# Attention: key rows loaded through GpSimd's queue, and a three-level split without GpSimd

## The reference, cut to what matters

```
# layer 0, 16 heads of 16, causal, S = 2048, batch 2
q, k, v = x @ Wq.T + bq, x @ Wk.T + bk, x @ Wv.T + bv
w = softmax(q k^T / sqrt(16) + alibi, causal);  y = w v;  x += y @ Wo.T + bo
# layer 1: two score maps per head
y = (softmax(q1 k1^T) - lam * softmax(q2 k2^T)) v;  y = layernorm per head;  x += y @ Wc
```

## Time and profile before

| | us |
|---|---|
| Time, median of 3 runs (lowest, highest) | 6747.85 (6737.48, 6751.71) |
| The profiled execution, its own time | 6750.49 |
| Its span in the trace | 6748.4 |
| PE, DVE, ACT, POOL busy | 5221.8, 3307.6, 2556.6, 1576.2 |

### The profile page before, as it was taken

The page is one execution under the profiler, slowest core; times in us unless marked ns, Lnnn a source line. Parts: engine busy times, 40 slices in busy tenths (PEclk is TensorE's granted clock), DMA queues, the critical chain, the costliest instruction groups (busy, mean ns, idle before and its releaser), DMA issues. The chain is left out here.

```text
span 6748.4 us, 94042 instructions
## 1 busy us (share of the span) xinstructions
PE 5221.8 (77%) x30108; PEld 2792.5 (41%) x30112; DVE 3307.6 (49%) x4783; ACT 2556.6 (38%) x5006; POOL 1576.2 (23%) x1276
## 2 busy tenths in 40 slices
PE   6566558888787566489968688888888888977997
PEld 3454223333225355248943233333323333344686
DVE  7411646666545621311157566666666666543011
ACT  2311116655561311122221265556555665612221
POOL 2488200000001288333323000000000001002332
PEclk9678769999898687789989699999999999988998
DMA  2476431112103277408945111111111111011498
GB/s 93 114 149 131 144 95 42 42 48 62 56 27 111 74 153 148 115 0 295 315 162 161 47 34 45 52 38 34 46 51 37 34 47 50 16 62 35 160 314 274
DMA packets 454295, 660.14 MB, mean 98 GB/s; under 512 B 97984, under 2 KB 308992, under 8 KB 448672
## 3 DMA queue, kind: packets, MB, share of 16 engines
q1 hardware_dynamic: 383232, 544.50, 25.8%
q0 software_dynamic: 70656, 110.44, 8.1%
HBM read 489.33 MB, written 164.20 MB: 97 GB/s over the span
## 5 line engine op out<-in xcount | busy, mean ns | idle before, releaser
L1670 DVE TENSOR_REDUCE ea_mx<-ea_psA 128x1 f32<-128x1024 f32 (+7 forms) x1280 | 1317.0, 1061 | 691.8 <-PE ea_psA L1535 484.4
L1652 ACT ACTIVATE ea_pr<-ea_psB 128x512 f32<-128x512 f32 (+3 forms) x2560 | 1229.5, 535 | 928.6 <-PE ea_psB L1557 508.1
L1532 PE MATMUL ea_psA<-ea_kx,ea_qx 99*128 99x512 bf16 (+3 forms) x2560 | 728.5, 362 | 284.3 <-DMA ea_kx<-in_c_k 255.0
L1670 DVE TENSOR_REDUCE ba_mx<-ba_psA 128x1 f32<-128x1024 f32 (+7 forms) x640 | 657.2, 1061 | 379.3 <-PE ba_psA L1535 279.9
L1557 PE MATMUL ea_psB<-ea_qx,ea_kx 99*128 99x512 bf16 (+3 forms) x2560 | 782.2, 354 | 29.1 <-issue 21.1
L1652 ACT ACTIVATE ba_pr<-ba_psB 128x512 f32<-128x512 f32 (+3 forms) x1280 | 610.7, 535 | 493.3 <-PE ba_psB L1557 259.4
L1572 PE MATMUL ea_psO<-ea_pr,ea_vx 128*32 128x512 f32 (+3 forms) x5120 | 610.5, 549 | 1.9 <-ACT ea_pr L1652 0.4
L1532 PE MATMUL ba_psA<-ba_kx,ba_qx 108*128 108x512 bf16 (+3 forms) x1280 | 370.5, 368 | 197.9 <-DMA ba_kx<-in_c_k 180.1
L1532 PEld LDWEIGHTS ea_psA<-ea_kx,ea_qx 99*128 99x128 bf16 x2560 | 217.5, 100 | 691.9 <-issue 378.5
L1504 POOL DMA_DIRECT2D ea_qx<-ea_mT x192 | 105.6, 557 | 1540.0 <-DVE ea_mT L1692 1515.8
L1557 PEld LDWEIGHTS ea_psB<-ea_qx,ea_kx 99*128 99x128 bf16 x2560 | 242.3, 99 | 500.9 <-ACT ea_pr L1652 315.0
(11 more groups left out here) (524 smaller groups left out, 8248.3 us busy)
## 6 DMA issues: line engine op xcount, KB each, us to landing
de_wg<-in_L_rg SPq DMA_DIRECT2D x64, 512.0 KB, 4.6
de_wu<-in_L_ru SPq DMA_DIRECT2D x64, 512.0 KB, 5.7
de_wd<-in_L_rd SPq DMA_DIRECT2D x64, 512.0 KB, 7.2
fe_wg<-in_L_rg SPq DMA_DIRECT2D x64, 512.0 KB, 4.6
fe_wu<-in_L_ru SPq DMA_DIRECT2D x64, 512.0 KB, 5.6
fe_wd<-in_L_rd SPq DMA_DIRECT2D x64, 512.0 KB, 7.0
ae_w<-in_L_w SPq DMA_DIRECT2D x64, 384.0 KB, 3.8
ce_w<-in_L_w SPq DMA_DIRECT2D x64, 384.0 KB, 3.5
```

The source lines that it names most:

```text
L1532: last = nc.tensor.matmul(psA[:, slot, at:at + n], qx[0:KB, s, hh, t * P:(t + 1) * P], kx[0:KB, s, hh, k:k + n], start=True, stop=not diag)
L1652: nc.scalar.activation(pr[:, j % 2, hh, off:BLK], psB[:, exp_slot(n, s), off:BLK], ACT.Exp).then_inc(s_exp, 1)
L1670: v.tensor_reduce(out, src, AX.X, ALU.max).then_inc(s_ar, 1)
```

## The change

Three edits.

1. The 14 key loads of a step (12 of levels, 2 of constants) leave SP and are issued by POOL, in the order 32, 16, 48 rows in each group. POOL issues them ahead of portion 1 of the step's maxima, behind the same wait for PE. SP issues all 14 query loads in one piece, then `vx`, then the inverses.
2. PE's one wait for both groups becomes one for the queries and one for the keys. The keys' semaphores now last over both attentions.
3. In the projections ACT reads `ps` twice, into `t32` and into the first level; DVE makes the remainder, the second level and the third. POOL does nothing there. ACT waits for the third level of two units earlier, where it waited for the second.

```
 # project_phase, ACT
-                    nc.scalar.activation(t32[:, k % 2, :], ps[:, k % 2, :], f, scale=mats[m][2],
+                    nc.scalar.activation(t32[:, k % 2, :], ps[:, k % 2, :], f, scale=mats[m][2], **a)
+
+                    act.wait_ge(s_out[k % NL], ((b * QB + i) * (nu // NL) + k // NL) * 16)
+                    nc.scalar.activation(lev[:, k % NL, 0], ps[:, k % 2, :], f, scale=mats[m][2],
 # project_phase, DVE
-                    nc.vector.tensor_copy(lev[:, v, 0], t32[:, u, :]).then_inc(s_c, 1)
+                    nc.vector.tensor_tensor(res[:, u, :], t32[:, u, :], lev[:, v, 0], ALU.subtract).then_inc(s_c, 1)
                     dve.wait_ge(s_c, base + n * 2 + 1)
-                    after(dve, s_lo, n, 2, first)
-                    nc.vector.tensor_tensor(res[:, u, :], t32[:, u, :], lev[:, v, 0], ALU.subtract).then_inc(s_c, 1)
+                    nc.vector.tensor_copy(lev[:, v, 1], res[:, u, :]).then_inc(s_c, 1)
                     dve.wait_ge(s_c, base + n * 2 + 2)
-                    nc.vector.tensor_copy(lev[:, v, 1], res[:, u, :]).then_inc(s_r, 1)
+                    nc.vector.tensor_tensor(lev[:, v, 2], res[:, u, :], lev[:, v, 1], ALU.subtract).then_inc(s_lo, 1)
 # attention_phase, SP
-                                sp.dma_start(kx[at:at + n * DH, s, hh, :], lk[0:n, rows, :]).then_inc(s_ld[s][g], 16)
...
                     if nxt:
                         if prev:
                             sp.wait_ge(s_av, st * NU)
-                        load(st + 1, 1 - s, 0)
+                        load_queries(st + 1, 1 - s)
                     if prev:
                         inverses_in(st - 1, 1 - s, use + s - 1)
-                    if nxt:
-                        load(st + 1, 1 - s, 1)
 # attention_phase, POOL
+                def load_keys(st, s):
+                    at = {3: F, 2: F + 3 * DH, 1: F + 5 * DH}
+                    for g in range(2):
...
+                        for n in (2, 1, 3):
+                            for h, hh in enumerate(range(HV)[own]):
+                                pool.dma_start(kx[at[n]:at[n] + n * DH, s, hh, :],
+                                               lk[0:n, r0 + h * DH:r0 + (h + 1) * DH, :]).then_inc(s_lk[s], 16)
...
                 def body(st, s, use, prev, nxt, before):
+                    if nxt:
+                        if prev:
+                            pool.wait_ge(s_av, st * NU)
+                        load_keys(st + 1, 1 - s)
                     store_maxima(st, s, 1)
```

More of the change, by code:

```diff
@@ L1109, in project_phase @@
         psV = sc.ps("psV", [P, 2, BLK])
-        s_w, s_vw, s_mm, s_t, s_c, s_r, s_lo, s_vm, s_vs, s_vi = (
-            sc.sem(n) for n in ("w", "vw", "mm", "t", "chain", "r", "lo", "vm", "vs", "vi"))
+        s_w, s_vw, s_mm, s_t, s_c, s_lo, s_vm, s_vs, s_vi = (
+            sc.sem(n) for n in ("w", "vw", "mm", "t", "chain", "lo", "vm", "vs", "vi"))
         s_out = [sc.sem(f"out{u}") for u in range(NL)]
@@ L1189, in scaled @@
                     act.wait_ge(s_mm, n + 1)
-                    after(act, s_r, n, 2, first)
+                    after(act, s_lo, n, 2, first)
                     a = {} if vbias is None else {"bias": bias[:, 2 * m + half:2 * m + half + 1]}
                     f = ACT.Copy if vbias is None else ACT.Identity
-                    nc.scalar.activation(t32[:, k % 2, :], ps[:, k % 2, :], f, scale=mats[m][2],
+                    nc.scalar.activation(t32[:, k % 2, :], ps[:, k % 2, :], f, scale=mats[m][2], **a)
+                    act.wait_ge(s_out[k % NL], ((b * QB + i) * (nu // NL) + k // NL) * 16)
+                    nc.scalar.activation(lev[:, k % NL, 0], ps[:, k % 2, :], f, scale=mats[m][2],
                                          **a).then_inc(s_t, 1)
@@ L1326, with attention_phase @@
 FIRST_MAXIMA = [e for i in range(CUT) for e in [("A", (0, i))] + [(k, (0, KIND_LAST.index(i))) for k in "LM" if i in KIND_LAST]]
-def attention_phase(nc, name, D, C, lvq, lvk, vd, yT, sums, sgn, maps, qc, kc, F, MR, s_m, st0):
+def attention_phase(nc, name, D, C, lvq, lvk, vd, yT, sums, sgn, maps, qc, kc, F, MR, s_m, st0, s_lk, lk0):
     two = maps == 2
@@ L1352, in attention_phase @@
         psO = sc.ps("psO", [P, BLK])
-        s_ld = [[sc.sem(f"ld{s}{g}") for g in range(2)] for s in range(2)]
+        s_lq = [sc.sem(f"lq{s}") for s in range(2)]
         s_v = [sc.sem(f"v{s}") for s in range(2)]
@@ L1423, in _, with load_queries @@
             def _(sp):
-                def load(st, s, *groups):
-                    for g in groups:
+                def load_queries(st, s):
+                    for g in range(2):
                         if two:
-                            lq, lk, r0, own = lvq[g], lvk[g], st * (2 * DH), slice(g, HV, 2)
+                            lq, r0, own = lvq[g], st * (2 * DH), slice(g, HV, 2)
                         else:
-                            lq, lk, r0, own = lvq[0], lvk[0], st * (HV * DH) + g * 2 * DH, slice(2 * g, 2 * g + 2)
+                            lq, r0, own = lvq[0], st * (HV * DH) + g * 2 * DH, slice(2 * g, 2 * g + 2)
                         at = F
@@ L1432, in load @@
                             for h, hh in enumerate(range(HV)[own]):
-                                rows = ds(r0 + h * DH, DH)
                                 sp.dma_start(qx[at:at + n * DH, s, hh, :],
-                                             lq[3 - n, rows, :].unsqueeze(0).broadcast_to((n, DH, S))).then_inc(s_ld[s][g], 16)
-                                sp.dma_start(kx[at:at + n * DH, s, hh, :], lk[0:n, rows, :]).then_inc(s_ld[s][g], 16)
+                                             lq[3 - n, ds(r0 + h * DH, DH), :].unsqueeze(0).broadcast_to((n, DH, S))
+                                             ).then_inc(s_lq[s], 16)
                             at += n * DH
[L1438 to L1445, removed]
+                        sp.dma_start(qx[0:F, s, own, :], qc.unsqueeze(1).broadcast_to((F, 2, S)) if shared else
+                                     qc[ds((st * HV + 2 * g) * F, 2 * F), :].rearrange("(h f) s -> f h s", h=2)
+                                     ).then_inc(s_lq[s], 16)
+                    sp.dma_start(vx[:, s].rearrange("p k c -> p (k c)"),
+                                 vd[ds(st, 1)].rearrange("g p c -> p (g c)")).then_inc(s_v[s], 16)
                 def sums_out(st, s, use):
@@ L1485, in body @@
                             result_out(st - 1, 1 - s, Q)
-                load(0, 0, 0, 1)
+                load_queries(0, 0)
                 steps_of(sp, body)
@@ L1505, in store_maxima @@
                                        mT[hh * 3 * tc:(hh + 1) * 3 * tc, k, :]).then_inc(s_m[k], 16)
+                def load_keys(st, s):
+                    at = {3: F, 2: F + 3 * DH, 1: F + 5 * DH}
+                    for g in range(2):
+                        if two:
+                            lk, r0, own = lvk[g], st * (2 * DH), slice(g, HV, 2)
+                        else:
+                            lk, r0, own = lvk[0], st * (HV * DH) + g * 2 * DH, slice(2 * g, 2 * g + 2)
+                        for n in (2, 1, 3):
+                            for h, hh in enumerate(range(HV)[own]):
+                                pool.dma_start(kx[at[n]:at[n] + n * DH, s, hh, :],
+                                               lk[0:n, r0 + h * DH:r0 + (h + 1) * DH, :]).then_inc(s_lk[s], 16)
+                        pool.dma_start(kx[0:F, s, own, :], kc.unsqueeze(1).broadcast_to((F, 2, S)) if shared else
+                                       kc[(st * HV + 2 * g) * F:(st * HV + 2 * g + 2) * F, :].rearrange("(h f) s -> f h s", h=2)
+                                       ).then_inc(s_lk[s], 16)
                 def scaled(st, s, use):
@@ L1580, in difference @@
                                      start=True, stop=True).then_inc(s_af, 1)
-                for g in range(2):
-                    pe.wait_ge(s_ld[0][g], 16 * nld)
+                pe.wait_ge(s_lq[0], 16 * nld)
+                pe.wait_ge(s_lk[0], 16 * (lk0 + nld))
                 n = 0
@@ L1613, in body @@
                                 arrived = True
-                                for g in range(2):
-                                    pe.wait_ge(s_ld[1 - s][g], 16 * nld * (use + s + 1))
+                                pe.wait_ge(s_lq[1 - s], 16 * nld * (use + s + 1))
+                                pe.wait_ge(s_lk[1 - s], 16 * nld * (use + s + 1) + 16 * lk0)
                             maxima(i, 1 - s if d else s, slot)
@@ L2029, in macaron_kernel @@
         s_g0, s_s0, s_g1, s_o1 = lasting("gather0_", RING), lasting("scatter0_", S0), lasting("gather1_", RING), lasting("scatter1_", NY1)
-        s_m = lasting("maxima", len(KINDS))
+        s_m, s_lk = lasting("maxima", len(KINDS)), lasting("keys", 2)
         with Scope(nc, "in") as si:
```

13 lines of the change are left out of this document (3 added, 10 removed).

## The result

The changed kernel takes 6426.07 us (median of 4 runs, 6409.67 to 6439.05) against 6744.48 us before on the same chip: a ratio of 0.953, 95% interval 0.9507 to 0.9552. It is 318 us faster; 6328 was forecast, in a range of 6255 to 6440. The direction and the mechanism hold, and a quarter of the forecast gain is missing. Its profiled execution took 6425.53 us, with a span of 6423.7.

What follows compares the result with a forecast made beforehand. PE bounds the kernel, apart from its stalls for late key loads. Terms of 127 (`ba`), 192 (`ea`), 48 (starts) and 52 (projections) sum to 419 us less, giving 6328 us, range 6255 to 6440.

Steps and rivals of the forecast that it cites:

- What bounds the kernel, and why the load is late: Steps of both attentions: PE stalls for group 1's keys, loaded after group 0 on two or three engines at 25 GB/s each.
- Steps of `ba`: Six steps of `ba`: PE's stall for the key load goes, 21.1 us per step, -127 us.
- Steps of `ea`: 14 steps of `ea`: stall goes, 2 us of new wait for POOL's multiply, 13.7 us per step, -192 us.
- Starts: Starts of the two attentions: PE waits for one group's worth plus 3 us for keys, 24 us saved twice, -48 us.
- if queries alone take much over 30 us: Sign of being wrong, while SP loads queries: they were forecast to land 27 to 30 us after SP's first issue.
- Projections: Projections in `ep`: DVE's subtractions take 0.69 us without POOL, 0.54 us less per unit over 96 units, -52 us.
- POOL's new work: POOL in the steps: 14 key DMAs of about 0.7 us ahead of maxima portion 1, 10 us to spare, 0 us.
- The range: Whole kernel: from the terms' bounds 6270 to 6400 us; the range holding 8 in 10 is 6255 to 6440.
- POOL's queue was no brake: Rival, POOL in the steps: key DMAs over about 1.5 us delay maxima portion 1; at 2 us, 6450 us; chance 0.10.
- The keys did leave the three engines: Rival, key loads: keys stay on the same three engines, nothing gained by the other queue, about 6860 us; chance 0.06.

Runs made afterwards that it cites:

- the two versions: Changed kernel with rows level beside level, keys on GpSimd's queue: 6274.74 us; kernel before with such rows, all loads on SP, new projections split: 6281.57 us.

## Why the prediction was right, and where it was off

- *What bounds the kernel, and why the load is late*: right. A share of 0.19 and 0.13 of 16 engines was three and two engines, and the version with an outer dimension of 16 on the same queue shows that this was the whole brake. By the Trainium skill ("DMA: Bandwidth & Descriptors", section "Why a DMA increments its semaphore by 16 and not by 1") such a DMA uses two or three engines, always the lowest-numbered on SP's queue, and neighbours from a cursor that moves round on GpSimd's. The shares agree with it, 0.20 with the queries alone and 0.67 to 1.10 with the keys on GpSimd's queue; the trace does not number the engines.
- *Steps of `ba`*: right, -124 for -127. The step that the rows showed is 110.0 us now; the six average 113.3, but they averaged 134.0 before, so the difference holds.
- *Steps of `ea`*: the mechanism was right (the first difference becomes the next to wait), the term mis-sized. I took 2 us of wait, at most 5; it is 5.0 us of idle time, and some 2 us more at the lower clock behind it. 124.65 - 117.5 = 7.2 us per step, 100 in all. The term that was mis-sized is the price of the keys on the shared engines, "2.5 to 5 us" less POOL's head start, worked out from shares of 64 KB at 25 GB/s. The multiply came 6.2 us later on average, with 1.2 to spare. The sum took an engine's rate for fixed. With nearly all engines at work it was 9 to 14 GB/s, for the queries too, and in six of 14 steps the sums' hop waited 4 to 7 us beside the keys. The term also rests on one step of 131.9 us, where the 14 averaged 133.5: without that the miss would be 22 us larger.
- *Starts*: -19 for -48, for the same reason. "One group's worth is half, 26.9, and the keys add 3" counts bytes on an engine and leaves out that its rate falls. 43.3 less 26.9 makes it about 16 for the keys. The prediction took it for a sign of being wrong "if queries alone take much over 30 us"; beside the keys they land 38.6 us after SP's first load. The start of `ea` was also 49.9 us before, not 53.8, so its half was worth less.
- *Projections*: right, DVE's subtraction is 0.69 us without POOL beside it; -57 for -52.
- *POOL's new work*: right, 0.6 us per DMA, no wait at slot 48.
- *The range*: its lower side adds 8, 28, 8 and 8 to 61, where they make 52; no conclusion hangs on it.
- *The rivals*: POOL's queue was no brake. The keys did leave the three engines. The Trainium skill's sentence that another issuer saves only issuing time ("DMA: Bandwidth & Descriptors", section "Issuing engines are not separate DMA queues") is borne out once the loads use 16 engines, 7 us between the two versions. On the change itself it was no guide: with loads on two or three engines each, the second queue alone gave 271 us.

## What to carry to other kernels

Read the DMA share as a number of engines: 0.19 and 0.13 under a long wait mean a transfer on three or two of 16, and the cure is its outer dimension, before any second queue. Reorder a contraction freely if it gives the load an outer dimension of 16; it cost nothing here and gained 403 us, against 271 for the second queue. When a long stall goes, price what comes next with the traffic that the cure sets free, and don't price shared engines by the rate that they had when few were at work.

## What the runs showed of the hardware that was not expected

- A DMA engine moved 25 GB/s in 4 KB rows with two or three at work, and 8 to 15 GB/s with nearly all 16 at work on loads of 16 to 48 partitions: 113 to 218 GB/s in total in the windows shown, and the same at both DRAM pitches tried.
- A subtraction of 128x512 f32 took 0.69 us on DVE alone and 1.52 us beside one on POOL. Two subtractions on DVE were cheaper than one on each engine.
